# AdaLN attention block on one core: the first tail tile's loads are issued inside the QKV stage, and the next batch's head tiles are normalised and scaled on ScalarE

## The reference, cut to what matters

```python
mod = (_silu(L0_c) @ L0_wmod).reshape(L0_c.shape[0], 6, 1, -1)
sa, ca, ga, sb, cb, gb = (mod[:, 0], mod[:, 1], mod[:, 2], mod[:, 3], mod[:, 4], mod[:, 5])
h = _layernorm(x, axis=-1) * (1 + ca) + sa          # "head"
...
qkv = x @ W_qkv + b_qkv                             # attention, with rotary q and k
att = jnp.einsum('bhqd,bhkd->bhqk', q, k) / jnp.sqrt(jnp.float32(HS))
att = jnp.where(causal, att, jnp.float32(-1000000000.0))
att = jax.nn.softmax(att, axis=-1)
y = jnp.einsum('bhqk,bhkd->bhqd', att, v)
...
x = x + ga * (y @ W_proj + b_proj)                  # "tail"
h = _layernorm(x, axis=-1) * (1 + cb) + sb
...
yn = (y - mu) * jax.lax.rsqrt(var + 1e-05) * ln_g + ln_b   # y is h here
...
x = x + gb * yn
```

## Time and profile before

| | us |
|---|---|
| median of three runs (3326.0 to 3330.2) | 3326.5 |
| the profiled execution: its time | 3331.65 |
| the profiled execution: span from first to last instruction | 3329.9 |
| busy in that span: PE / DVE / ACT / POOL | 3022.2 / 2585.6 / 1759.3 / 1575.2 |

### The profile page before, as it was taken

How to read it: one execution, slowest core, us unless ns; L and a number is a source line. 1 busy time by engine, 2 the same in 40 slices (tenths; PEclk the granted TensorE clock), 3 DMA queues, 4 the chain that set the end, 5 groups by cost and what they waited for, 6 DMA issues and landing times.

```text
span 3329.9 us, 59017 instructions
## 1 busy us (share of the span) xinstructions
PE 3022.2 (91%) x21664; PEld 1154.2 (35%) x21664; DVE 2585.6 (78%) x4454; ACT 1759.3 (53%) x3411; POOL 1575.2 (47%) x1489
## 2 busy tenths in 40 slices
PE   3799999999989999999998999999898999999895
PEld 1323333324343433424333242433324333242221
DVE  4697777897768788897877878798776878878477
ACT  3416565656655555655455555565544555555551
POOL 2304343471616365372644726365471655627354
PEclk8759999999999999999999999999999999999997
DMA  5402030313041220413123041311314112031122
GB/s 207 106 10 66 20 69 19 92 39 75 13 103 39 70 57 23 100 39 84 39 52 93 26 94 33 80 50 39 87 33 109 42 45 72 26 77 45 48 75 69
DMA packets 180874, 205.27 MB, mean 62 GB/s; under 512 B 21460, under 2 KB 137428, under 8 KB 179428
## 3 DMA queue, kind: packets, MB, share of 16 engines
q1 hardware_dynamic: 180584, 201.50, 23.0%
HBM read 114.09 MB, written 36.50 MB: 45 GB/s over the span
## 4 chain that ended last, share of the span: by engine, by line
PE 46%; DVE 20%; issue 16%; POOL 6%; POOLq 5%; DVEq 3%; DMA 2%; ACT 1%; SPq 1%; ACTq 0%
DVE mpart L864 11%; PE ring L1108 9%; PE ps_out L1158 9%; PE ps_scores L1144 7%; PE ps_scores L1082 6%; PE ps_den L1175 4%; PE ps_scores L1094 3%; PE ring L1130 3%; PE ps_den L1181 3%; POOL psum L504 3%; DVE dsum L880 2%; POOL psum L503 2%; DVE wk L908 1%; POOLq L484 1%; DVE wk L906 1%
## 5 line engine op out<-in xcount | busy, mean ns | idle before, releaser
L699 ACT ACTIVATE prob<-ps_scores 128x512 f32<-128x512 f32 (+3 forms) x2560 | 1261.8, 537 | 1128.8 <-PE ps_scores L1147 548.6
L864 DVE TENSOR_REDUCE mpart<-ring 128x1 f32<-128x512 f32 (+3 forms) x2560 | 1399.4, 599 | 277.2 <-PE ring L1108 143.0
L1108 PE MATMUL ring<-qk 96*128 96x512 f16 (+3 forms) x2560 | 877.6, 364 | 91.0 <-DVE mpart L864 79.1
L1144 PE MATMUL ps_scores<-qk 98*128 98x512 f16 (+3 forms) x2560 | 865.5, 352 | 35.5 <-ACT prob L699 31.5
L503 POOL TENSOR_TENSOR psum<-prob 128x512 f32<-128x512 f32 x360 | 482.4, 1340 | 427.3 <-ACT prob L699 296.3
L1158 PE MATMUL ps_out<-prob,v 128*32 128x512 f32 (+3 forms) x5120 | 608.0, 547 | 0.0
L1108 PEld LDWEIGHTS ring<-qk 96*128 96x128 f16 x2560 | 235.7, 97 | 909.8 <-DVE mpart L864 666.7
L504 POOL TENSOR_TENSOR psum<-prob 128x512 f32<-128x512 f32 x360 | 481.8, 1338 | 0.0
L1144 PEld LDWEIGHTS ps_scores<-qk 98*128 98x128 f16 x2560 | 246.5, 98 | 347.0 <-ACT prob L699 213.1
L1082 PE MATMUL ps_scores<-hT,wg 128*128 128x512 f16 x1536 | 345.2, 382 | 3.5 <-POOL hT L494 3.5
L522 POOL TENSOR_TENSOR xs<-xs,bc 128x512 f32<-128x512 f32 x60 | 77.1, 1286 | 553.7 <-DMA xs<-in_L_attn_x_dram 552.8
(11 more groups left out here) (122 smaller groups left out, 2568.2 us busy)
## 6 DMA issues: line engine op xcount, KB each, us to landing
qk<-half SPq DMA_DIRECT2D x384, 128.0 KB, 3.5
turn<-in_rope_dram SPq DMA_DIRECT2D x64, 512.0 KB, 4.6
xs<-in_L_attn_x_dram SPq DMA_DIRECT2D x124, 256.0 KB, 2.8
attn_out_T<-ot SPq DMA_DIRECT2D x63, 256.0 KB, 2.1
otin<-attn_out_T SPq DMA_DIRECT2D x30, 512.0 KB, 4.7
out_dram<-x SPq DMA_DIRECT2D x60, 256.0 KB, 2.1
wg<-w_qkv_halves SPq DMA_DIRECT2D x16, 768.0 KB, 5.6
qk<-in_L_wmod_dram SPq DMA_DIRECT2D x1, 6144.0 KB, 26.7
```

What stands on the lines that cost most here:

```text
L699: act.activation(prob[:, s % 3, p, h % 2, 0:w], ps_scores[(HG * s + h) % NBK][:, 0:w], ACT.Exp, scale=SCALE).then_inc(exp_done, 1)
L864: dve.tensor_reduce(mpart[:, h, qt, kc:kc + 1], ring[n % NBK][:, 0:w], AX.X, ALU.max).then_inc(ring_free, 1)
L1108: mm = pe.matmul(ring[n % NBK][:, 0:w], qk[0:R, G % 2, 0, h, qt * P:(qt + 1) * P], qk[0:R, G % 2, 1, h, kc * QC:kc * QC + w], start=True, ...
L1144: mm = pe.matmul(ps_scores[k % NBK][:, 0:w], qk[0:RM, par, 1, h, kt * P:(kt + 1) * P], qk[0:RM, par, 0, h, cq * QC + q0:(cq + 1) * QC], st ...
```

## The change

SP issues the loads of the tail tile at step 2 inside the QKV stage, at its third chunk, ahead of the load of the tables for the fourth chunk. In a head group, normalising and scaling go from DVE to ACT. For it POOL also computes the shift -mean/deviation (two more small instructions a tile). The 4 scalings stand one step later than before, between the first and the second exponent, and normalising stands between the third and the fourth exponent of the step ahead of the transpose. `head_low` stands one step later. `vector_load` no longer counts these two for DVE, which moves the row-maximum tiles between steps in the head groups only. The bank that a scaling frees is told on a semaphore of ACT (`bank_free`), and the position in the ring is carried through all batches.

```diff
+    FIRST_TAIL = 2
...
-        return load + 2.7 * (s in head) + 2.2 * (s + 2 in head) + (s + 1 in head)
+        return load + 2.2 * (s + 2 in head)
...
-            def qkv(G, before):
+            def qkv(G, before, tail_load):
                 for c in range(NC_):
                     if c > 0:
                         stack_halves(G, c - 1, 1)
+                    if c == 2:
+                        tail_load()
                     if G < NG * B - 1 or c < NC_ - 1:
                         load_turn(NC_ * G + c + 1)
...
-                        qkv(NG * b + g + 1, NG * b + g)
+                        qkv(NG * b + g + 1, NG * b + g, lambda: tail_load(FIRST_TAIL))
...
-                        if s + 2 in tail:
-                            t = tail[s + 2]
...
+                        if s + 2 != FIRST_TAIL:
+                            tail_load(s + 2)
...
             def head_tile(b, t):
                 pool.wait_ge(head_stat, NT * b + t + 1)
-                inv_std(rstd[:, t % 2, :], mv[:, t % 2, :]).then_inc(head_rstd, 1)
+                inverse = inv_std(rstd[:, t % 2, :], mv[:, t % 2, :])
+                if b == 0:
+                    inverse.then_inc(head_rstd, 1)
+                else:
+                    pool.tensor_tensor(shift[:, t % 2, :], mv[:, t % 2, 0:1], neg_one[:], ALU.mult)
+                    pool.drain()
+                    pool.tensor_tensor(shift[:, t % 2, :], shift[:, t % 2, :], rstd[:, t % 2, :], ALU.mult).then_inc(
+                        head_rstd, 1)
...
-                        if s - 1 in head:
-                            head_low(b + 1, head[s - 1])
+                        if s - 2 in head:
+                            head_low(b + 1, head[s - 2])
...
+                            if h == 0 and s - 1 in head:
+                                head_evac(b + 1, head[s - 1], turns[s - 1])
+                            if h == 2 and s + 1 in head:
+                                head_normed(b + 1, head[s + 1])
...
+            def head_normed(b, t):
+                act.wait_ge(head_rstd, NT * b + t + 1)
+                if t == 0 and b > 1:
+                    act.wait_ge(tail_done, NT * (b - 2) + 2 * T0)
+                act.activation(wk[:, t % 2, :], xs[:, t % 2, :], ACT.Identity, bias=shift[:, t % 2, :],
+                               scale=rstd[:, t % 2, :]).then_inc(head_norm, 1)
+
+            def head_evac(b, t, use):
...
+                act.wait_ge(head_done, NT * b + t - 1)
+                act.wait_ge(ring_full, use + 1)
+                for k in range(KC):
+                    scaled = act.activation(x1[:, t % 2, k * P:(k + 1) * P], ring[use % NBK][:, k * P:(k + 1) * P],
+                                            ACT.Identity, bias=colmod[:, 0, k:k + 1], scale=colmod[:, 1, k:k + 1])
+                scaled.then_inc(turn_free, 1)
+                act.drain().then_inc(head_scaled, 1)
...
-            def head_evac(b, t, use, n):
...
-                for k in range(KC):
-                    normed = dve.tensor_scalar(h32[:, k, :], src[:, k, :], colmod[:, 1, k:k + 1], colmod[:, 0, k:k + 1],
-                                               ALU.mult, ALU.add)
...
-                        if s + 1 in head:
-                            head_normed(b + 1, head[s + 1])
...
-                        if s in head:
-                            head_evac(b + 1, head[s], base + n, bank0 + n)
-                            n += 1
...
+            def bank_free(use):
+                if use >= NBK and freed_by[use - NBK] == "dve":
+                    pe.wait_ge(ring_free, freed[use - NBK])
+                elif use >= NBK:
+                    pe.wait_ge(turn_free, NT + freed[use - NBK])
```

More of the change, by code:

```diff
@@ L260, in job_base @@
             return NT // 2 if isinstance(b, int) and b == 0 else NT * b
-        def ring_base(b):
-            return NS * HG if isinstance(b, int) and b == 0 else NS * HG + RING * b - NT
-        def ring_first(b):
-            return ring_base(b if isinstance(b, int) and b == 0 else 1) % NBK
-        assert RING % NBK == 0
+        freed_by = ["dve"] * (NS * HG)
+        for b in range(B):
+            for g in range(NG):
+                last = b == B - 1
+                tail, head, own = tail_at(g, b == 0, last), head_at(g, last), own_at(g, last)
+                plan = unit_plan(tail, head)
+                for s in range(NS):
+                    freed_by += ["dve"] * (0 if last and g == NG - 1 else len(plan[s]))
+                    freed_by += ["dve"] * ((s in tail) + (s in own)) + ["act"] * (s in head)
+        freed_by += ["dve"] * TPC
+        counts = {"dve": 0, "act": 0}
+        freed = []
+        for who in freed_by:
+            counts[who] += 1
+            freed.append(counts[who])
         assert NC_ == 4 and NBK == 3
@@ L277, in batches @@
         def batches(body):
-            for b in range(B - 1):
-                body(b, first=b == 0, last=False)
-            return body(B - 1, first=False, last=True)
+            n = NS * HG
+            for b in range(B):
+                n = body(b, b == 0, b == B - 1, n)
+            return n
         block = ctx.enter_context(nc.Block())
@@ L397, in end_attention, with body, tail_load @@
                     ot_ld[t // 2 % 2], 16)
-            def body(b, first, last):
+            def body(b, first, last, n):
                 for g in range(NG):
+                    tail, head, own = tail_at(g, first, last), head_at(g, last), own_at(g, last)
+                    def tail_load(at):
+                        if at in tail:
+                            t = tail[at]
+                            Z = NT * (b - 1) + t
+                            if t < 2 or (t < 2 * T0 + 2 and t >= 2 * T0 and not last):
+                                tail_loads(b - 1, t, head_norm, NT * (b + 1 + (t > 1)))
+                            else:
+                                tail_loads(b - 1, t, tail_done, Z - 1)
                     if last and g == NG - 1:
@@ L407, in body @@
                         load_group((g + 2) % NG)
-                    tail, head, own = tail_at(g, first, last), head_at(g, last), own_at(g, last)
                     for s in range(NS):
@@ L562, in _, with body @@
             pool.drain().then_inc(scale_rows, 1)
-            def body(b, first, last):
+            def body(b, first, last, n):
                 jobs = job_base(b)
-                n = 0
-                bank0 = ring_first(b)
                 for g in range(NG):
@@ L685, in body @@
                         maxima(G)
+                    tail, head, own = tail_at(g, b == 0, last), head_at(g, last), own_at(g, last)
+                    plan = unit_plan(tail, head)
+                    turns = {}
                     for s, (cq, kt) in enumerate(STEPS):
@@ L688, in body @@
                         S = NS * G + s
+                        n += (len(plan[s]) if nxt else 0) + (s in tail) + (s in own)
+                        if s in head:
+                            turns[s] = n
+                            n += 1
                         for h in range(HG):
@@ L702, in body @@
                                 high(G + 1, NC_ - 1, h // 2)
-                        if s - 1 in head_at(g, last):
-                            head_high(b + 1, head_at(g, last)[s - 1])
-                        own = own_at(g, last)
+                            if h == 0 and s - 1 in head:
+                                head_evac(b + 1, head[s - 1], turns[s - 1])
+                            if h == 2 and s + 1 in head:
+                                head_normed(b + 1, head[s + 1])
+                        if s - 1 in head:
+                            head_high(b + 1, head[s - 1])
                         out = leaving(s, "leave", bool(own))
@@ L892, in tail_product @@
                     dve.wait_ge(tail_done, NT * b + t - 1)
-                dve.tensor_tensor(wk[:, t % 2, :], ring[n % NBK][:, :], bc[:, 0, :], ALU.mult).then_inc(ring_free, 1)
+                if t in (2 * T0, 2 * T0 + 1) and b < B - 2:
+                    dve.wait_ge(head_scaled, NT * (b + 2))
+                dve.tensor_tensor(wk[:, t % 2, :], ring[use % NBK][:, :], bc[:, 0, :], ALU.mult).then_inc(ring_free, 1)
             def tail_stage(b, t, stage):
```

102 lines of the change are left out of this document (45 added, 57 removed).

## The result

The changed kernel takes 3283.5 us (median of 4 runs, 3277.6 to 3289.8) against 3328.4 for the kernel before beside it (3326.0 to 3331.1): ratio 0.9865, 95% interval 0.9843 to 0.9887. The gain is 45 us where 64 was forecast.

A forecast was written before the change was run, and what follows sets the result against it. PE bounds plain groups; in head groups DVE is fullest. Early loads (54.1 - 12.9 - 1.5 = 39.7 us) plus the head (24) take 64 us off 3326.5, giving 3263 us; range for 8 in 10: 3242 to 3291.

The forecast's parts named there:

- The waits removed: Tail groups: early loads end step 3's excess wait (46.9 us) and the groups 1's late `out_high` (7.2), together 54.1 us.
- In a group 0 all three loads stand ahead, 6.2 us, and the tables come 4.3 us late.: End of QKV stage: loads delay the tables, less 1.9 us slack; 12.9 us lost over three groups, at worst 7.9 each.
- a tables' wait that spreads into steps 0 to 2: Sign in the groups' first steps: if the wait for the tables spreads there, the prediction is wrong.
- three issues cost SP little: SP's queue: issuing the three loads takes 0.37, 0.56 and 0.60 us; the 4.18 of `xs` was called a full queue.
- They land in the order of issue.: DMA queue: `bv`, `bc`, `otin`, `xs` land in that order; in a busy queue `bc` adds 3.8 us, `otin` 1.8, `xs` 0.7.
- Half a microsecond in each of the groups with `otin` and `xs`: Three groups loading these two alone: 2.4 us of delay less the tables' slack leaves 0.5 each, together 1.5 us.
- Rival 2: Wait moves to the end of the QKV stage: `bc` delays the tables, groups 0 win nothing; 3282 us, chance 0.10.
- The head: Head groups: DVE no longer the bound, PE's 145.8 us is; 8 us gained of a possible 12.7, 24 in three groups.
- rival 3: Head groups: ACT takes DVE's place as the bound, gain only 0.8 us each; 3284 us, chance 0.14.
- two other banks and three score tiles: Ring on PE: a transpose's bank waits for ACT's scaling, but PE has these before needing it; no cost counted.
- The prediction's sign for the bank: Head groups: if PE's transposed bank is waited for at every tile, the prediction is wrong.
- Rival 5: Slower: ACT's added 36.3 us lies in series with PE's work in head groups, 182 us each; 3357 us, chance 0.06.

The follow-up runs named there:

- tail_ahead: The changed kernel with the first tail tile's loads issued in the last step of the group before, ahead of the QKV stage; 3252.1 us.
- tables_first: The changed kernel with the same three loads issued behind the fourth chunk's tables instead of ahead of them; 3276.2 us.
- norm_dve: `tail_ahead` with normalising back on VectorE and POOL's two shift instructions gone, the scalings staying on ScalarE; 3251.0 us.
- head_only: The changed kernel with the tail tile's loads put back into the steps, normalising and scaling staying on ScalarE; 3312.1 us.
- scale_first: `tail_ahead` with the four scalings on ScalarE ahead of the step's first exponent instead of behind it; 3253.1 us.

## Why the prediction came out as it did

**The waits removed.** Right. Step 3 waits 3.71 us in (1,0), and 1.25 us is left of `out_high` in (1,1). `tail_ahead`, where nothing is given back, shows the size: 60.6 us for 54.1.

**"In a group 0 all three loads stand ahead, 6.2 us, and the tables come 4.3 us late."** The step that failed, in size. Counted from the first exponent of step 0 to that of step 2, the groups 0 give back 8.8 us in (1,0), 8.2 in (2,0) and 9.7 in (3,0): 26.7 for 12.9, above the end of 7.9 each. That leaves 32.2 - 26.7 = 5.5 us (measured over the whole groups: 6.8). By the prediction's own sign, a tables' wait that spreads into steps 0 to 2, this term was wrong. Three things make up the difference.

The transfers themselves were sized about right: in (1,0) the tables take 5.8 us more from issue to landing (10.5 for 4.7), where 6.2 was added; in (2,0) and (3,0) it is 3.2 and 7.4. But they are also issued 3.7 us later (4.4 and 2.1 in the other two), since SP issues the loads first and stands, in (1,0), 0.53, 0.55 and 2.40 us at them. The prediction put this term at nothing ("three issues cost SP little") and set the 4.18 us of `xs` in the earlier trace rows aside. So the rotation comes 7.6 us late for the 4.3 counted, and 5.9 and 7.8 in the other two.

The stackings behind the tables take 8.7 us for 3.8, and `high` waits for them as well. In (1,0) both waits end together, as the prediction's "until about the same time" has it, and `tables_first` shows that the second is nearly enough by itself. `high` comes 6.2, 4.9 and 5.8 us late in the three groups, 16.9 together.

The other 9.8 us lie behind `high`, in steps 0 and 1, where the granted clock is 0.50: each of the three groups has a stretch of 10.2 us, most of it behind the wait. The prediction has no term for the clock. That the low clock makes up these 9.8 us is read from the traces and not from a run that kept the wait alone.

**"They land in the order of issue."** Not refuted, and not all of it can be seen. Each of these transfers raises its semaphore in sixteen steps, and the three stackings of a half raise the same one, so the trace does not tell which of them a step belongs to. What it shows is that a transfer can be late in a few of its parts: before the change the tables' sixteen steps came between 952.0 and 952.3, after it twelve between 951.6 and 951.8 and the last four between 953.0 and 955.2. The Trainium skill says in "DMA: Bandwidth & Descriptors", section "Two DMAs through the same engine are not ordered", that nothing orders transfers across the 16 DMA engines. The trace agrees: twelve steps of the stackings behind the tables came between 952.5 and 952.8, ahead of those last four.

**Half a microsecond in each of the groups with `otin` and `xs`.** Also low: steps 0 and 1 give back 1.9, 1.5 and 1.7 us in (1,3), (2,3) and (3,2). These three give 11.0 us for the 12.9 + 1.8 - 1.5 = 13.2 forecast. The groups 1 give 7.5 for 7.2, and one of them, (3,1), pays 4.0 us in steps 0 and 1 that were counted as nothing: DVE waits 3.44 us for the tables there, `high` comes 0.4 us late, and the granted clock is 0.50 for 6.8 us behind it.

**Rival 2** named this: the wait moves to the end of the stage. Its mark, a wait of over 8 us for the tables, is there (9.31), and its 3282 us is nearly the time measured. It is not quite the case, since the groups 0 gain 6.8 us and not nothing, but most of their gain did go this way; 0.10 was too little for it. That 3282 is so near is luck in part: it has 24 us for the head, which brought 14 by itself. The prediction's words against it, "more than any row has", were about rows in which nothing so large stood ahead of the tables.

**The head.** 8 us a group were forecast, 5.2 came (15.5 in three), and of these 2.1 (6.3 in three) lie in steps 0 and 1, which hold no head tile. Two things differ there. PE has 3 and 3 score tiles for the next group's row maxima, before 4 and 5. And in (1,2) and (2,2) the kernel before has a stretch of 3.4 us at the granted clock 0.50 in step 1, which is gone; (0,2) has none there, before or after. (0,2) gains 1.05 us in these steps and the other two 2.6 each, so some 1.6 us in each of the two go with the clock. DVE's 113 came out as 116.6, ACT's 131 as 123.5. ACT's rows in (1,2), groups of instructions with busy us, mean ns, idle before:

```profile
L764 ACT ACTIVATE x<-ring,colmod 128x128 f32<-128x128 f32 x64 | 24.1, 468 | 0.0
...
L753 ACT ACTIVATE wk<-xs,shift,rstd 128x512 f32<-128x512 f32 x16 | 13.0, 814 | 2.1 <-POOL shift L513 2.1
```

The scalings take 24.1 / 16 = 1.5 us a tile, as worked out; the normalising 0.81 for the 0.69 taken. The reason given for stopping short of 12.7 was that ACT is full. Its account does close that way (123.5 busy, 26.9 idle before exponents, 2.1 before the normalising), but `norm_dve` takes 9 us off ACT and gains nothing, so a full ACT (rival 3) by itself is not the cause. Three of the four scalings are worth 3.4 us of the missing 7.5; whether through the ring bank, which the prediction had covered by "two other banks and three score tiles", or through ACT's time, is not separated, and the rest stays open. The prediction's sign for the bank is there: for 16 tiles weight loads wait for it 15 times (14.8 us), though matmuls only 7 times (4.0 us).

The Trainium skill, "ScalarE: Activation LUTs", section "Rules for kernel authors", would have multiplications and additions on VectorE. Here it decides nothing for the normalising (`norm_dve` 3251.0, `tail_ahead` 3252.1) and loses for the whole head, which is 14 us faster on ScalarE (`head_only`): VectorE was the fullest engine of that group. Rival 5 (ACT in series with PE) did not come.

## What to carry to other kernels

A load issued early is free only if nothing behind it in its queue is due soon. Count what stands behind it, for every waiter, by the bytes ahead and by the time that the issuing engine stands at its issues, and choose a place where nothing behind it is due: the same loads cost the groups 0 about 9 us each in the QKV stage and nothing a stage earlier, though the tables behind them are late there too. Read the granted clock behind a wait of PE: here more than a third of the loss (9.8 of 26.7 us) came after the wait had ended, most of the way at 0.50. An engine that is full by its account is not the bound until taking work off it shortens the stage. And a wait that gets shorter has not been won until the stage does: weight loads wait beside running matmuls, and in `scale_first` one wait of the matmuls was traded for another.

## What the runs showed of the hardware

Behind 2.3 MB of loads, a table of 512 KB took 10.5 us instead of 4.7, twelve of its sixteen parts being there after 7.0; SP's issue of `xs` took 2.40 us where `otin` took 0.55. While PE stood for 7.10 us the granted clock fell to 0.50, where a score matmul took 0.61 us instead of 0.38. An ACTIVATE of 128x512 from `xs`, with scale and bias per partition, took 0.81 us where one from `ps_scores` with a bias took 0.69.
